# The short group of four items moved from the front of the edge pass to its end

## The reference, cut to what matters

```
Wx = x @ Ws[h] + Wb[h]
s  = leaky_relu(Wx[v_tgt] @ a_w[h, :d] + Wx[v_src] @ a_w[h, d:] + a_b[h], 0.2)
alpha = segment_softmax(s, v_tgt)
out_h = segment_sum(alpha[:, None] * Wx[v_src], v_tgt)
```

## Time and profile before

| what | value |
|---|---|
| median of 3 runs | 2387.91 us (2383.07, 2387.91, 2393.5) |
| span of the profiled execution | 2392.9 us |
| TensorE, VectorE, ScalarE, GpSimd busy | 84%, 59%, 43%, 43% of the span |
| the pass over the edges, first gather to last add | 152.3 to 768.2 us |

### The profile page before, as it was taken

How to read it: one execution, slowest core, us unless ns; L and a number is a source line. 1 busy time by engine, 2 the same in 40 slices (tenths; PEclk the granted TensorE clock), 3 DMA queues, 4 the chain that set the end, 5 groups by cost and what they waited for, 6 DMA issues and landing times. The chain is left out here.

```text
span 2392.9 us, 35675 instructions
## 1 busy us (share of the span) xinstructions
PE 2009.4 (84%) x8716; PEld 1279.8 (53%) x8716; DVE 1416.6 (59%) x3001; ACT 1020.9 (43%) x3220; POOL 1027.6 (43%) x1051
## 2 busy tenths in 40 slices
PE   5957888888887625259999999897899999999998
PEld 4745666666665313124433444354346888888544
DVE  6646888988888762476666656577852222222343
ACT  2325777777776603465666656344001111111000
POOL 1037777777772404257777777300001111111331
PEclk9978999999999657779999999999999999999999
DMA  5547888888883734777777777785316999999652
GB/s 147 124 151 240 243 246 237 244 239 241 244 235 94 287 107 99 192 249 223 224 224 225 223 223 225 246 283 180 123 53 214 361 368 365 366 366 364 226 191 88
DMA packets 276214, 537.31 MB, mean 225 GB/s; under 512 B 43507, under 2 KB 121947, under 8 KB 275859
## 3 DMA queue, kind: packets, MB, share of 16 engines
q0 software_dynamic: 80544, 261.97, 37.4%
q1 hardware_dynamic: 177043, 240.65, 29.5%
q10 hardware_dynamic: 18464, 32.84, 4.0%
HBM read 449.56 MB, written 86.57 MB: 224 GB/s over the span
## 5 line engine op out<-in xcount | busy, mean ns | idle before, releaser
L852 POOL DMA_INDIRECT g_G<-tab,src_of_item x440 | 445.6, 1013 | 178.6 <-issue 109.1
L917 PE MATMUL g_psA<-g_G,g_oh 128*128 128x261 f32 x1760 | 444.1, 399 | 61.7 <-DVE g_G L1067 48.7
L1222 PE MATMUL g_psA<-g_G,g_oh 128*128 x832 | 387.5, 608 | 76.2 <-SPq L1178 69.0
L1162 POOL DMA_INDIRECT g_G<-tab,src_of_tile x392 | 371.0, 946 | 165.7 <-issue 82.0
L974 ACT ACTIVATE g_G<-g_G 128x64 f32<-128x64 f32 x1760 | 425.1, 336 | 0.0
L1265 DVE TENSOR_TENSOR acc<-acc,g_psA 128x512 f32 x416 | 285.7, 687 | 186.1 <-PE g_psA L1222 145.4
L917 PEld LDWEIGHTS g_psA<-g_G,g_oh 128*128 128x128 f32 x1760 | 327.0, 194 | 125.5 <-DVE g_G L1067 62.4
L1222 PEld LDWEIGHTS g_psA<-g_G,g_oh 128*128 128x128 f32 x832 | 146.4, 190 | 294.4 <-issue 293.1
L2441 PE MATMUL mo_bank<-mo_xT,mo_w 128*128 128x128 f32 x2304 | 269.1, 275 | 0.3 <-ACT mo_xT L2478 0.3
L2344 POOL DMA_INDIRECT mo_g<-tab,mo_slot x72 | 68.1, 946 | 456.9 <-PE mo_bank L2431 325.0
L2441 PEld LDWEIGHTS mo_bank<-mo_xT,mo_w 128*128 128x128 f32 x2304 | 263.0, 192 | 1.0 <-ACT mo_xT L2478 0.5
(11 more groups left out here) (425 smaller groups left out, 2532.4 us busy)
## 6 DMA issues: line engine op xcount, KB each, us to landing
mo_w<-in_L_ffn_w SPq DMA_DIRECT2D x216, 512.0 KB, 8.5
ys<-mo_y ACTq DMA_DIRECT2D x72, 256.0 KB, 5.6
g_ot<-reld SPq DMA_DIRECT2D x27, 512.0 KB, 5.8
ys<-sg_zeros SPq DMA_DIRECT2D x24, 512.0 KB, 4.5
g_G<-tab,src_of_item POOLq DMA_INDIRECT x440
g_pen<-pend SPq DMA_DIRECT2D x216, 32.0 KB
tab<-fi_row SPq DMA_DIRECT2D x25, 261.0 KB, 2.7
xmid<-at_x SPq DMA_DIRECT2D x25, 256.0 KB, 5.1
```

Of the source, the lines that this page charges most:

```text
L852: q.indirect_dma_start(G[:, j % RING, :], None, tab0, bass.IndirectOffsetOnAxis(K.src[:, j:j + 1], 0)).then_inc(gs[g % 3], 16)
L917: ins = tens.matmul(psA[u][:, f, 0:HW], oh[:, n % OR, h, :], G[:, r + h, f * HW:(f + 1) * HW], start=(h == 0), stop=(h == SUP - 1))
L1162: g.indirect_dma_start(G[:, (j + 1) % MR, :], None, table, bass.IndirectOffsetOnAxis(K.src1[:, j:j + 1], 0)).then_inc(got[j % MR], 16)
L1222: tens.matmul(psA[n % MB][:], oh[:, n % MO, :], G[:, ds(tile1 % MR, 1), :].rearrange("p o d -> p (o d)"), start=True, stop=True).then_inc( ...
```

## The change

```diff
-GI = (4,) + (8,) * 27
+GI = (8,) * 27 + (4,)
 GS = tuple(sum(GI[:j]) for j in range(len(GI) + 1))
...
     def step_of(g, k):
-        return min(GS[g] - min(6, GI[g - 1] - 1) + k, GS[g] - 1)
+        return min(GS[g] - (3 if g == NG - 1 else 6) + k, GS[g] - 1)
```

## The result

The changed kernel takes 2398.05 us against 2388.29 us, medians of ten runs each: ratio 1.0039, interval 1.0026 to 1.0051, which is 6 to 12 us slower. The forecast had been 2391.2 us, in a range of 2382 to 2401.

What follows compares the result with a forecast made beforehand. The prediction took GpSimd's gather stream, ending at 731.65, plus a tail to bound the pass. Tail terms moved the last add from 768.2 to 771.5, so 2387.9 + 3.3 = 2391.2 us, range 2382 to 2401.

Steps and rivals of the forecast that it cites:

- The stream: GpSimd's 440 gathers in the pass over the edges: no stop before or after the change, 0 us.
- The last gather: End of gather 440, closing the gather stream: expected at 731.65 again, as before the change.
- The sign: Stated mark of a wrong forecast: a last gather more than 3 us from 731.65.
- The front: Start of the pass: group 0 needs 16 gathers, item 0 is prepared some 11 us later, cost 0.
- The slack: Early items are summed before gathers need their ring slots, with at least 5 us to spare.
- Rival B: Ring fills at the front as TensorE's clock stays low, stopping gathers about 11 us: 2402 us; chance 0.08.
- Rival C: Items set the groups' pace, so item 0's 11 us later start reaches the end: 2399 us; chance 0.04.
- L1008 for group 26: VectorE's last wait for gathers, ahead of item 202: at 724.7 (723.5 to 725.6), 4.0 us landing after gather 432.
- the sum: Tail terms added from the wait at 724.7 to the last add at 771.5, against 768.2 before: +3.3 us.
- The squeezed chain: Last group's serial steps from turned carries to scaling ahead of item 215: TensorE idle about 4.2 us.
- Items 215 to 219 with the factors: TensorE's end of the pass: 5 x 1.824 + 0.76 = 9.9 us, to 770.6.
- Rival A: Tail shortens, the last group's half-width steps fitting beside the items: end at 766.3, time 2386 us; chance 0.17.

Runs made afterwards that it cites:

- all groups five ahead: Changed kernel with every group's steps five items ahead, so weights and hand-out fall together ahead of item GS-1: 2469.01 us, ratio 1.0337 to the kernel before.
- the long front alone: Kernel before with groups of 8, 4, then 26 times 8, the last group's steps standing where they stood: 2388.95 us, ratio 1.0005.
- the filled kernels: Changed kernel with extra TensorE products ahead of item 215, 12 or 10 behind the turned weights: 2397.64 and 2394.18 us, ratios 1.0031 and 1.0026 to before.
- the six-ahead kernel: Changed kernel with the last group's steps six items ahead, not three, run twice: 2393.27 us in the first; ratios 1.0017 and 1.0032 to before.
- the split tail: Kernel before with groups of 4, 26 times 8, 4, 4, one group more, the last short with squeezed steps: 2399.69 us, ratio 1.0042.
- the squeezed long group: Kernel before, groups unchanged, with the steps of the last group of 8 three items ahead: 2391.68 us, ratio 1.0021.
- the four-ahead kernel: Changed kernel with the last group's steps four items ahead, not three: 2396.22 us, ratio 1.0027 to the kernel before.

## Why the prediction was right, and where its size was off

- *The stream bounds the pass, and runs without a stop.* Right. In thirteen of the fourteen profiles no gap between gathers exceeds 0.35 us; only with all groups five ahead does the stream stop.
- *The last gather at 731.65, the last add near 771.* They came at 724.79 and 765.95. The prediction had called a last gather more than 3 us from 731.65 a sign that it was wrong. The sign was badly chosen: a second profile of the kernel before has it at 725.18, because the pass begins at another time in each run. Only differences within the pass can be held against the forecast.
- *The front costs nothing.* Right in the tail and the gaps: the changed kernel's own stream never stops, and the long front alone has ratio 1.0005. The slack was as forecast: item 2 was done at 197.03 and its gather came at 203.87, item 4 at 202.84 and its gather at 208.90. Rival B's mechanism did not come: the granted clock was 0.50 up to 187, 1.00 in 188 to 194 and 0.50 again in 195 to 197, so item 2 was slow too, but it was back by item 3, as these rows of the changed kernel's TensorE show (items 0 and 1, 2, 3), which answer to the earlier trace rows:

```profile
183.28 5.71 PE L917 MATMUL g_psA<-g_G,g_oh 128*128 128x261 f32 x16
...
193.60 3.43 PE L917 MATMUL g_psA<-g_G,g_oh 128*128 128x261 f32 x8 [0.80 <-DVE g_G L1067]
...
197.25 2.04 PE L917 MATMUL g_psA<-g_G,g_oh 128*128 128x261 f32 x8
```

- *Rival C* fell with the same run: item 0 starts later, and nothing is carried. That the measured 2398 us lie next to C's 2399 is chance, and that they lie inside the range at all is partly luck, since its upper end had been drawn for C and most of B.
- *L1008 for group 26 lands 4.0 us behind gather 432.* It was 717.46 - 714.62 = 2.84, the lower end. Against the last gather's end it was 7.33 us early, where the sum had 6.95.
- *The squeezed chain, 4.2 us of idle TensorE.* It was 1.48 + 2.26 = 3.7. From L1054 to item 215 it was 3.21, forecast 3.33.
- *Items 215 to 219 with the factors, 9.9 us.* This term was mis-sized: 11.6, 11.6 and 13.9 us in three profiles, because the idle time just ahead of them lowers TensorE's clock. The sum took the term from the earlier trace rows, where nothing stood idle, although had in the same line a first item of 2.83 us behind a 2.32 us gap. Without the low clock the forecast tail, 771.5 - 731.65 = 39.85 us, is what the filled kernels have: 39.5 and 39.9.
- *Rival A* needed the short group's steps to fit beside the items. Even with six items of room the tail is 37.2 to 37.5, not the 34.65 that its end at 766.3 means.

The tail thus accounts for 4.6 to 6.9 us of the loss, 3.3 of which were forecast. The timed loss is 9.3 us by the first ratio and about 8 by the two others. Some 1 to 5 us are missing, and not only here: in every altered kernel (all five ahead aside) the timed loss is 1 to 7 us above what its tail shows, most in the six-ahead kernel (tail +0.7, timed +4 and +8, whose intervals begin at +1.4 and +4.5 us), and 2 to 3 us in the split tail and the squeezed long group, whose fronts are as before. The cause stays open. The stream gives a hint and no more: it took 578.9 us on average in nine profiles that begin with a group of 8 (576.1 to 581.4; all five ahead left out), and 576.9 in four that begin with one of 4 (575.4 to 579.4). The ranges overlap, and the kernels with the front as before, which miss some us too, are among the short ones. The stretch ahead of the pass varied from 147.3 to 154.2 us between profiles, so one profile for each kernel can't settle it.

Nor did timing confirm the low clock's part, or that undoing the squeeze gains; only the traces show both. Taken together: the late start of item 0 is shown to stop no gather and to lengthen no tail, the reordering with its squeeze is shown to lengthen the tail by 4.6 to 6.9 us, the squeeze alone is shown in the traces to cost 4 to 6 us of it (1.6 to 3.9 by the clock), and the rest of the timed loss is open.

## What to carry to other kernels

Where the start of a stage hides under a stream that bounds it and the end doesn't, look first at what a reordering moves to the end. Here the short group's squeezed steps cost nothing at the front and 4 to 6 us at the end, and even with six items of room the group did not shorten the tail (37.2 and 37.5 us against 36.6 and 36.7). When a chain over four engines is put ahead of one instruction, price not only the idle time but also the matmuls behind it, at the lower clock. And a distance that hides a chain should not be shortened without a look at its last link: here the chain one item later, with its last two steps in one place, cost 80 us over 27 groups.

## What the hardware showed that was not expected

Behind an idle stretch of TensorE of some 2.3 us its granted clock fell from 2.4 to 1.2 GHz in all three profiles of the changed kernel, with another stretch of 1.48 us and one transpose ahead of it, and in the four-ahead kernel, with only 0.66 us ahead. Its means were 0.85 and 0.71 over the 11.7 and 14 us that followed. With no gap over 0.65 us there the items kept their 1.83 us. The same idle stretch did not always bring the clock down: with all groups five ahead it came 27 times, and twice the item behind it took 2.00 us, at a granted clock of 1.00. How long the clock stayed low differed between runs of one kernel as well: for most of item 215 and the first factor product in two profiles, into item 216 in the third. The Trainium skill, "TensorE: Matmul & The Clock Gate", section "Part 1: The HAM clock gate", has the clock halved when the engine is idle and restored by sustained work; the traces agree on both.
